# Middle stage of an audio tower: banded filter rows stored 128 columns wide and loaded in two halves, gate and expert weights loaded a stage earlier, packs last, triangular systems in thirds

## What is computed

```
# layer 1: attention of each block with itself
probs = softmax(x @ x.T / 16);   h = probs @ x
# layer 2: h = h + attn(layernorm(h)); 4 heads of 64, chunks of 32 tokens
q, k, v = silu(causal_dwconv(xn @ W, 4 taps));   beta = sigmoid(xn @ Wb)
A = tril(kb @ k.T, -1);  T = inv(eye(32) + A);  u = T @ v_b;  w = T @ kb     # per chunk
# delta rule over the chunks of a sequence with a 64x64 state S
fir_short = causal_dwconv(v, 3 taps);   fir_long = causal_dwconv(v, 63 taps)
gates = softmax(mlp(concat(xn, mean and std of the four branches)))
o = gates . (fir_short, fir_long, delta_out, v);  o = rmsnorm(o) * w;  h += o @ Wo
# layer 3: h = h + ffn(layernorm(h)); 6 experts 256 -> 128 -> 256, top 2 of a router
```

## Time and profile before

| | us |
|---|---|
| median of 3 runs | 2713.1 (2710.72 to 2714.3) |
| the profiled execution, its own time | 2711.45 |
| its span, first to last instruction | 2709.7 |
| PE busy | 2412.4 (89%) |
| DVE busy | 1929.9 (71%) |
| ACT busy | 1377.0 (51%) |
| middle stage, first DMA issue to the first product of the third stage | 764.45 to 932.67 |

### The profile page before, as it was taken

How to read it: one execution, slowest core, us unless ns; L and a number is a source line. 1 busy time by engine, 2 the same in 40 slices (tenths; PEclk the granted TensorE clock), 3 DMA queues, 4 the chain that set the end, 5 groups by cost and what they waited for, 6 DMA issues and landing times.

```text
span 2709.7 us, 53423 instructions
## 1 busy us (share of the span) xinstructions
PE 2412.4 (89%) x21052; PEld 1817.1 (67%) x21052; DVE 1929.9 (71%) x5233; ACT 1377.0 (51%) x2633; POOL 537.6 (20%) x373
## 2 busy tenths in 40 slices
PE   4888888888889689999999999999999999999997
PEld 3666666666568566677767777776777677777764
DVE  3888898998859246667767776777676667656655
ACT  3777777777734224444454444445444544454442
POOL 0333333333310001111111111111111111111111
PEclk9998999999987568999999999999999999999999
DMA  2666666666679702223212221322132223212200
GB/s 79 194 206 204 202 202 207 205 219 206 199 281 345 259 19 90 69 68 112 68 62 102 102 68 62 103 77 68 66 111 89 68 71 109 68 62 92 85 18 18
DMA packets 223162, 334.47 MB, mean 123 GB/s; under 512 B 113857, under 2 KB 190625, under 8 KB 213697
## 3 DMA queue, kind: packets, MB, share of 16 engines
q1 hardware_dynamic: 219744, 309.03, 34.3%
q10 hardware_dynamic: 2304, 12.58, 1.2%
q0 software_dynamic: 864, 9.44, 0.9%
HBM read 191.68 MB, written 164.23 MB: 131 GB/s over the span
## 4 chain that ended last, share of the span: by engine, by line
PE 40%; DVE 16%; ACT 6%; issue 3%; POOL 0%; DVEq 0%
PE bank L1543 6%; PE bank L1474 5%; PE bank L1533 5%; PE bank L1366 4%; PE bank L1485 3%; DVE DL L1875 3%; PE bank L1504 3%; ACT L1680 3%; DVE v_all L1961 3%; PE bank L1478 2%; PE bank L1397 2%; PE bank L1405 2%; PE bank L1452 1%; DVE e L1920 1%; ACT HE L1680 1%
## 5 line engine op out<-in xcount | busy, mean ns | idle before, releaser
L704 DVE SCALAR_TENSOR_TENSOR Y<-bank,convw,Y 128x383 f32<-128x383 f32 (+2 forms) x576 | 314.4, 605 | 7.0 <-ACT Y L580 7.0
L1543 PE MATMUL bank<-w2e,HE 128*128 128x256 f32 x1152 | 289.9, 388 | 12.1 <-DVE v_all L1961 9.2
L1961 DVE SCALAR_TENSOR_TENSOR v_all<-bank,we,v_all 128x256 f32<-128x256 f32 x576 | 242.7, 476 | 79.2 <-PE bank L1543 76.9
L432 PE MATMUL bank<-pb,wqkv 128*128 128x384 f32 x768 | 284.9, 501 | 10.6 <-issue 10.5
L1533 PE MATMUL bank<-v_all,w1e 128*128 128x384 f32 x768 | 285.8, 495 | 1.4 <-ACT HE L1680 1.4
L1841 DVE TENSOR_TENSOR L<-bank,b2g 128x48 f32<-128x48 f32 x32 | 6.6, 208 | 343.7 <-PE bank L1485 343.7
L1543 PEld LDWEIGHTS bank<-w2e,HE 128*128 128x128 f32 x1152 | 208.0, 192 | 49.5 <-issue 16.6
L1474 PE MATMUL bank<-v_all,w1g 128*128 128x384 f32 x512 | 201.8, 517 | 0.4 <-ACT v_all L1672 0.4
L1680 ACT ACTIVATE HE<-bank 128x384 f32<-128x384 f32 x192 | 94.3, 491 | 194.6 <-PE bank L1533 193.8
L432 PEld LDWEIGHTS bank<-pb,wqkv 128*128 128x128 f32 x768 | 137.4, 196 | 83.0 <-issue 24.6
L804 POOL TENSOR_TENSOR RR<-RS,minus_half 128x24 f32<-128x24 f32 x32 | 133.3, 4165 | 267.9 <-DVE RS L753 267.9
(11 more groups left out here) (211 smaller groups left out, 5342.2 us busy)
## 6 DMA issues: line engine op xcount, KB each, us to landing
packa<-pa SPq DMA_DIRECT2D x32, 1932.0 KB, 8.1
v_all<-packa SPq DMA_DIRECT2D x32, 1932.0 KB, 7.8
packb<-pb SPq DMA_DIRECT2D x32, 768.0 KB, 5.9
v_all<-packb SPq DMA_DIRECT2D x32, 768.0 KB, 6.9
toeplitz<-taps SPq DMA_DIRECT2D x128, 190.0 KB, 4.9
toep<-toeplitz SPq DMA_DIRECT2D x32, 760.0 KB, 9.4
packb<-fsk SPq DMA_DIRECT2D x32, 384.0 KB, 2.3
first_stage<-fl SPq DMA_DIRECT2D x32, 384.0 KB, 5.5
```

The costliest lines, as they stand in the source:

```text
L432: mm = pe.matmul(proj_bank[j][:, 0:T], wqkv[:, a, j * P:(j + 1) * P], xnT[:, a, :], start=(a == 0), stop=(a == HALF - 1))
L704: dve.scalar_tensor_tensor(out=Y[:, j, lag:T], in0=proj_bank[j][:, 0:T - lag], scalar=convw[:, j, CK - 1 - lag:CK - lag], in1=Y[:, j, lag: ...
L1543: mm = pe.matmul(expert_bank(b), HE[k % 2][:, b * P:(b + 1) * P], w2e[:, k, :], start=True, stop=True)
L1961: dve.scalar_tensor_tensor(out=HA[s][:, b, :], in0=expert_bank(b), scalar=we[s][:, b, k:k + 1], in1=HA[s][:, b, :], op0=ALU.mult, op1=ALU. ...
```

## The change

- `toeplitz` holds 128 instead of 190 columns a row. A row p below 64 keeps the first 128 columns of its window, one from 64 on the last 128 (the columns left out hold zeros there).
- Each filter group is loaded by two DMAs, 64 rows each: rows 0 to 63 to columns 0 to 127 of `toep`, rows 64 to 127 to columns 62 to 189. Columns 0 to 61 of rows 64 to 127 are cleared once by four DVE memsets, for which PE waits before its first group. The product with the last 62 columns uses rows 64 to 127 alone.
- `w1g` (512 KB) and the six parts of `w1e` (128 KB each) are allocated ahead of the first stage and loaded in its first seven steps that have a sequence c.
- `load_packs` stands behind the last filter load.
- Each set of systems is loaded by three DMAs of 512 KB, issued at given values of `solve_step`; set 0 by three in a row. The stores stay whole.
- A semaphore that nobody waited for (`v_kept`) goes.

```diff
--- before.py
+++ after.py
@@ -99,7 +99,7 @@
             "systems": nc.dram_tensor("systems", [NB * NM * NQ, SC, SC], F32, kind="Internal").ap(),
             "fl": nc.dram_tensor("fl", [NH, P, NB * BLK * DH], F32, kind="Internal").ap(),
             "taps": nc.dram_tensor("taps", [D, 512], F32, kind="Internal").ap(),
-            "toeplitz": nc.dram_tensor("toeplitz", [P, D, TW], F32, kind="Internal").ap(),
+            "toeplitz": nc.dram_tensor("toeplitz", [P, D, P], F32, kind="Internal").ap(),
         }
         c = ctx
         bank = banks()
@@ -113,8 +113,9 @@
         shared = dict(expanded=expanded, NB=NB, dram=dram, bank=bank, ident=ident, upper=upper)
         make_constants(nc, ctx, ident, upper)
         v_all = sb("v_all", [P, D, BLK * NB])
-        first_phase(nc, x, w, shared, v_all)
-        third_phase(nc, w, out, shared, third_phase_weights(nc, ctx), v_all)
+        early = early_weights(nc, ctx)
+        first_phase(nc, x, w, shared, v_all, early)
+        third_phase(nc, w, out, shared, third_phase_weights(nc, ctx, early), v_all)
 
 
 def make_constants(nc, ctx, ident, upper):
@@ -145,7 +146,7 @@
                 sp.sem_inc(g.sem, g.per * g.primed)
 
 
-def first_phase(nc, x, w, shared, v_all):
+def first_phase(nc, x, w, shared, v_all, early):
 
     NB, dram, bank, ident, upper, expanded = (shared[k] for k in ("NB", "dram", "bank", "ident", "upper", "expanded"))
     with ExitStack() as c:
@@ -258,7 +259,6 @@
         kbT0_copied = signal("kbT0_copied")
         kbT1_copied = signal("kbT1_copied")
         at_copied = signal("at_copied", 2)
-        v_kept = signal("v_kept")
         prime(nc, signals)
 
         proj_bank = [bank[n] for n in (3, 4, 5, 3, 4, 5)]
@@ -345,13 +345,22 @@
 
                     for k in range(P // NB):
                         p = c * (P // NB) + k
-                        sp.dma_start(dram["toeplitz"][p], dram["taps"][:, bass.ds(P - 1 - p, TW)]).then_inc(expanded, 16)
+                        sp.dma_start(dram["toeplitz"][p], dram["taps"][:, bass.ds(P - 1 - p + (p // DH) * (FL - 1), P)]).then_inc(expanded, 16)
+
+                def load_early(c):
+                    if c == 0:
+                        sp.dma_start(early["w1g"][:, :, :], w["mlp_w1"][0:D].rearrange("(a p) n -> p a n", a=HALF))\
+                            .then_inc(early["early_loaded"], 16)
+                    elif c <= NE:
+                        sp.dma_start(early["w1e"][:, :, c - 1, :], w["ffn_w1"][c - 1].rearrange("(a p) n -> p a n", a=HALF))\
+                            .then_inc(early["early_loaded"], 16)
 
                 def body(a=None, b=None, c=None, s=0, ahead=True):
                     if a is not None and ahead:
                         load_x(a + 1, 1 - s)
                     if c is not None:
                         expand(c)
+                        load_early(c)
                     if b is not None:
                         store_h(b, 1 - s)
                     if c is not None:
@@ -369,6 +378,7 @@
                 body(NB - 1, NB - 2, NB - 3, 1, ahead=False)
                 body(b=NB - 1, c=NB - 2, s=0)
                 body(c=NB - 1, s=1)
+                sp.wait_ge(early["early_loaded"], 16 * (1 + NE))
                 for s in range(2):
                     sp.wait_ge(*pack_stored[s].before(NB // 2))
                     sp.wait_ge(*h_stored[s].before(NB // 2))
@@ -812,8 +822,7 @@
 
                         pool.wait_ge(*vtok_copied.now(c))
                         for b in range(BLK):
-                            keep = pool.tensor_copy(v_all[:, :, c + b * NB], toks(pa[s], VTOK)[:, b, :])
-                        keep.then_inc(v_kept.sem, 1)
+                            pool.tensor_copy(v_all[:, :, c + b * NB], toks(pa[s], VTOK)[:, b, :])
                     if a is not None:
                         inverse_std(a)
 
@@ -826,11 +835,19 @@
                 body(c=NB - 1, s=1)
 
 
-def third_phase_weights(nc, ctx):
+def early_weights(nc, ctx):
     def sb(name, shape):
         return ctx.enter_context(nc.sbuf_tensor(name, shape, F32))
 
-    w1g = sb("w1g", [P, HALF, MLP])
+    return dict(w1g=sb("w1g", [P, HALF, MLP]), w1e=sb("w1e", [P, HALF, NE, DE]),
+                early_loaded=ctx.enter_context(nc.semaphore("early_loaded")))
+
+
+def third_phase_weights(nc, ctx, early):
+    def sb(name, shape):
+        return ctx.enter_context(nc.sbuf_tensor(name, shape, F32))
+
+    w1g, w1e = early["w1g"], early["w1e"]
     w1s = sb("w1s", [P, MLP])
     b1g = sb("b1g", [P, MC])
     w2g = sb("w2g", [P, MC, 4 * NH])
@@ -840,7 +857,6 @@
     router = sb("router", [P, HALF, NE])
     anchors = sb("anchors", [P, NE, ND])
     rclip = sb("rclip", [P, 1])
-    w1e = sb("w1e", [P, HALF, NE, DE])
     w2e = sb("w2e", [P, NE, D])
     itemp = sb("itemp", [P, NH])
     loaded = ctx.enter_context(nc.semaphore("p3_weights"))
@@ -864,28 +880,24 @@
     if n == 2:
         load(tail["wo"][:, :, :], w["Wo"].rearrange("(a p) n -> p a n", a=HALF))
     if n == 3:
-        load(tail["w1g"][:, :, :], w["mlp_w1"][0:D].rearrange("(a p) n -> p a n", a=HALF))
-    if n == 4:
         load(tail["w1s"][0:GATE_S, :], w["mlp_w1"][D:])
         load(tail["w2g"][:, :, :], w["mlp_w2"].rearrange("(m p) n -> p m n", m=MC))
-    if n == 5:
+    if n == 4:
         load(tail["b2g"][:, :], w["mlp_b2"].partition_broadcast(P))
         load(tail["anchors"][:, :, :].rearrange("p e d -> p (e d)"), w["ffn_anchors"].rearrange("e d -> (e d)").partition_broadcast(P))
-    if n == 6:
+    if n == 5:
         with nc.allow_non_contiguous_dma(reason="a few columns, once"):
             load(tail["b1g"][:, :], w["mlp_b1"].rearrange("(m p) -> p m", m=MC))
-    if n in (7, 8):
+    if n in (6, 7):
         with nc.allow_non_contiguous_dma(reason="a few columns, once"):
-            load(tail["router"][:, n - 7, :], w["ffn_proj_w"][:, (n - 7) * P:(n - 6) * P].rearrange("e p -> p e"))
-    if 9 <= n < 9 + NE:
-        load(tail["w1e"][:, :, n - 9, :], w["ffn_w1"][n - 9].rearrange("(a p) n -> p a n", a=HALF))
-    if n == 9 + NE:
+            load(tail["router"][:, n - 6, :], w["ffn_proj_w"][:, (n - 6) * P:(n - 5) * P].rearrange("e p -> p e"))
+    if n == 8:
         load(tail["w2e"][:, :, :], w["ffn_w2"].rearrange("e p n -> p e n"))
 
 
-WEIGHT_LOADS = 18
+WEIGHT_LOADS = 11
 CLEARED = 3 + 7
-CONSTANTS = 2 + NE - 1
+CONSTANTS = 2 + NE - 1 + 4
 
 
 def second_phase(nc, w, shared, v_all, stage, tail, solve, load_packs, load_factors):
@@ -907,7 +919,7 @@
         toep = [sb(f"toep{s}", [P, CG, TW]) for s in range(NT)]
         solve["X"][0] = sb("X0", [P, SG, SC, SC])
         GI = DH // CG
-        toep_loaded = [signal(f"toep_loaded{s}", 16) for s in range(NT)]
+        toep_loaded = [signal(f"toep_loaded{s}", 32) for s in range(NT)]
         fl_ready = signal("fl_ready", 2, primed=2)
         fl_copied = signal("fl_copied", 2, primed=2)
         prime(nc, signals)
@@ -923,15 +935,16 @@
                 for it in range(groups):
                     if it >= NT:
                         sp.wait_ge(*fl_ready.now(it - NT))
-                    sp.dma_start(toep[it % NT][:, :, :], dram["toeplitz"][:, it * CG:(it + 1) * CG, :])\
-                        .then_inc(toep_loaded[it % NT].sem, 16)
+                    for half in range(2):
+                        rows = slice(half * DH, (half + 1) * DH)
+                        sp.dma_start(toep[it % NT][rows, :, half * (FL - 1):half * (FL - 1) + P],
+                                     dram["toeplitz"][rows, it * CG:(it + 1) * CG, :]).then_inc(toep_loaded[it % NT].sem, 16)
                     if it == NT:
                         for g in tail["signals"]:
                             sp.sem_inc(g.sem, g.per * g.primed)
                     if it > NT:
                         load_third_phase_weight(nc, sp, w, tail, it - NT - 1)
-                    if it == groups - 6:
-                        load_packs(sp)
+                load_packs(sp)
                 load_factors(sp, setup_act)
                 sp.wait_ge(loaded, 16 * WEIGHT_LOADS)
 
@@ -944,6 +957,7 @@
                                   v_all[:, D - 5 * (k + 1):D - 5 * k, :].rearrange("p c n -> p (c n)"), start=True, stop=True)
 
                 dense(5)
+                pe.wait_ge(setup, CONSTANTS)
                 for i in range(0, groups // NT):
                     for s in range(NT):
                         it = i * NT + s
@@ -959,8 +973,8 @@
                                           start=(k == 0), stop=False, skip_group_check=True)
                             for k in range(4):
                                 ch, o = half * 4 + k, k * BLK * NB
-                                mm = pe.matmul(acc[0:TW - P, o + NB:o + BLK * NB], toep[s][:, ch, P:],
-                                               v_all[:, it * CG + ch, 0:(BLK - 1) * NB],
+                                mm = pe.matmul(acc[0:TW - P, o + NB:o + BLK * NB], toep[s][DH:P, ch, P:],
```

(27 more changed lines are left out.)

## The result

The changed kernel takes 2724.1 us (median of 5 runs, 2719.87 to 2727.97); before takes 2713.1 (5 runs, 2708.77 to 2714.3). The ratio is 1.0043, with a 95% interval of 1.0028 to 1.0057. The change makes the kernel slower, by 11.0 us from median to median and 11.7 by the ratio, where 38 us of gain were forecast. The profiled execution took 2727.97 us, 16.5 more than that of before: 4.0 in the first stage (the middle stage begins at 768.45, before at 764.45), 8.4 in the middle stage, 4.2 from the third stage's start on.

A forecast was written before the change was run, and what follows sets the result against it. PE's middle stage was held to lose 42.2 us to two filter-load stalls and their half-clock stretches; with PE ending at 889 and the third stage starting at 895, 37.7 us earlier, 2711.45 became 2673.8, predicted 2675 us, range 2663 to 2700.

The forecast's parts named there:

- Filter rows: Middle-stage filter loads: 1,024 pieces of 512 bytes at 28.7 ns, 1.84 us a group instead of 2.08.
- ledger of 103.9 us: Middle stage: DMA work up to the last filter load, 122.5 us before, 103.9 after; unstalled PE leaves 115.7.
- tight stretch: Middle stage, 790 to 833: DMA work fills 42.6 of 43 us; PE may run dry once, 4 us allowed.
- the cover is 18 us for 7.4 us of data: Middle stage's end: packs issued 13 us ahead of PE's end, needed 5 us behind it; otherwise first products wait some 5 us.
- Packs last: Middle stage: packs behind the last filter load remove SP's 14.3 us wait and 7.4 us of DMA ahead of load 27.
- rival e: Gain given back, for instance by packs or factors that land late: within 0.2% of before; chance 2%.
- the forecast's 895: Start of the third stage, taken as the later of ACT's 894.4 and DVE's 894.1; 37.7 us ahead of 932.67.
- Rival (b): Filter loads: 512-byte pieces cost 47 ns, also for 128 KB HBM stride; third stage at 921, gain 12, 2701 us; 9%.
- Rival (a): Middle stage: PE runs dry more often, one full half-clock stretch and some 5 us of stalls; gain 24, 2689 us; 20%.
- Rival (c): Middle stage: 64-row products let TensorE's clock fall; 2.68 us lost per half-clock group, 2757 us with all 32; 7%.
- the +2 us for the thirds: Middle stage: set 0 in three loads lets DVE end 2 us later, at 893.6; start up to 1 earlier or 5 later.
- A rule against the change: DMA queues take equal turns by piece, so 512-byte filter loads get almost nothing while a set or `fl` store runs.

The follow-up runs named there:

- one_load: Changed kernel with one 128-partition filter load into columns 0 to 127 instead of two of 64 partitions (filter result displaced); 2693.55 us, ratio 0.9924 to before.
- packs_last_only: Kernel before with only the packs moved behind the last filter load; 2692.88 us, ratio 0.9926 to before.
- hbm_stride: Changed kernel with a partition's filter rows 131,584 instead of 131,072 bytes apart in HBM; 2716.23 us, ratio 1.0006 to before.
- wide_whole: Kernel before with only early weights and packs last (190-column filter rows, whole systems); 2686.70 us, ratio 0.9898 to before.
- wide_factors_first: Changed kernel with 190-column filter rows in one load, 128-row products, and factor loads issued ahead of the packs; 2688.50 us, ratio 0.9916 to before.
- deferred: Kernel before with early weights and packs last, plus the fourth systems set and some factor loads moved to the third stage; 2682.14 us, ratio 0.9869.
- two_queues: Changed kernel with filter rows 64 to 127 loaded by ACT on its own queue, SP keeping rows 0 to 63; 2704.50 us, ratio 0.9968 to before.
- halves_only: Kernel before with only the new filter rows (128 columns, two 64-row loads, memsets, 64-row product); 2731.27 us, ratio 1.0066 to before.
- early_only: Kernel before with only the weights loaded in the first stage; 2703.92 us, ratio 0.9976 to before.

## Why the prediction was wrong

**The step that failed is the price of a 512-byte piece**, under "Filter rows": 28.7 ns, 1.84 us a group, "as source and target are of the kind of the large loads". Measured: 41.9 ns, 64 x 41.9 = 2.68 us a group, more than the 2.08 of the wide rows that it replaces. It lay inside the bounds named, 21.9 and 47 ns, but the choice between them looked at bytes and memories and not at which partitions a load touches. The runs show that as the cause: the same pieces cost 29.3 ns when one load covers 128 partitions, 41.9 when loads of 64 come one after the other on a queue, 36.3 when two queues serve the halves; stride and alignment leave 42.2 and 40.1. The estimate of 28.7 was right for loads of 128 partitions, and the trace of before could have shown it: beside other sizes it holds 1,536 pieces of 512 bytes, the loads of `w1e` to 128 partitions, at 27.0 ns on the mean. The Trainium skill states the mechanism ("SBUF — State Buffer", Door 1: The DMA port swizzle): partition bit 6 selects which of two ports of a cluster is used, so 64 neighbouring partitions reach 8 of the 16 ports. Half of the 436 GB/s that the page gives is 218; the trace agrees, with 16 x 512 bytes / 41.9 ns = 196 GB/s and the 180 of the first window. The same page of the Trainium skill ("Can I just issue two DMAs to hit both halves?") says that two concurrent DMAs at partitions 0 and 64 were only 6% faster than a single one. Here two queues against one queue made the pieces 13% shorter, 36.3 against 41.9 ns. No run here counts ports, so that the limit is the ports is the page's reading and not shown.

The half-wide loads slow the others too: up to PE's end POOL's 4,096-byte pieces took 215 ns in the changed kernel and 185 in one_load, the pieces of ACT's stores (6,144 bytes) 299 and 247. The ledger of 103.9 us becomes 32 x 2.68 + 45 = 131 with the first alone, above the 122.5 of before and above the 115.7 that PE needs. The tight stretch, which the prediction saw as "42.6 of 43 us", was then far over: the stall came at the second group, and all else of the PE timeline follows. Unstalled PE would have taken from 775.5 to 889; it took 41.7 us longer, of which the three stalls are 6.8. 11 groups at half clock (7, 2 and 2, by 41.8, 12.0 and 11.6 us between stall and next `dense`) at up to 2.68 us too much are 29, and the `dense` at the end of each stretch, 5.17, 4.72 and 3.94 us instead of 2.52, are 6.3; together 42.

**The second failed step is "the cover is 18 us for 7.4 us of data"** under "Packs last". The data were covered: the first product never waited for `packa`. What was not counted is what stands behind the packs in SP's list. The chance for a gain given back by late packs or factors was put at 2% (rival e), without its price: 8 issues that took 6.3 us before take 23.67 behind packs and slow filter loads, and the third stage starts 14.35 us behind PE, not 5.4 or the forecast's 6. Yet the move itself gains 20 us, as packs_last_only shows; that part of the forecast was right in sign and in cause. In all, the third stage started 50.0 us behind the forecast's 895: 4.0 from the first stage, 37.7 from PE's slower filters and 8.3 from the pause behind them.

**Rival (b)** named the right term, with 47 ns for 41.9, but at 2701 us the wrong sum and, with HBM rows 128 KB apart, the wrong mechanism (hbm_stride). It counted one half-clock stretch where there were three, no slowing of other queues, and the old tail. **Rival (a)** is the way in which PE was hit, short stalls that each cost a stretch. **Rival (c)** fell as it was put: no stretch of 0.50 in the middle stage begins without a stall ahead of it, full clock holds from 828 to 848 and 903 to 931 on filter products alone, and 8 of the short products take 0.66 us, before 0.67. The clock is lost by stalls of 1.67 us as by ones of 10 us. Not every short stall costs it, and here a weaker form of (c) stays open. Where the last products had 128 rows, stalls of 1.35 us (wide_whole), 1.45 and 1.61 (wide_factors_first) left the clock at 1.00, and 1.93 (deferred) and 2.15 (wide_whole) did not. Where they had 64, stalls of 1.15 (one_load) and 1.50 us (two_queues) were already followed by 0.50 (though an idle time of 2.80 us right behind the first `dense` of halves_only was not). So the 64-row products may make the clock easier to lose; no run changes them alone.

Right were: the duration of the 64-row products; 3.31 and 5.99 us a group; DVE not being what ends the stage. The 3.5 us of DMA that the early weights free fit the 6.5 us of early_only, but its interval takes in no gain as well. DVE began `X0` at 778.64, 10.2 us behind the stage's start against 11.5 before, so that the +2 us for the thirds did not show here (with wide rows they cost 4); but it then waited 10.59 us for a constant that ACT makes when PE has done 8 groups, and ended at 904.9 instead of 893.6.

**Open.** The 4.0 us of the first stage: packs_last_only, which changes nothing there, begins its middle stage at 768.98, hbm_stride at 769.39, early_only at 766.42. So the change is not needed for them; that there is only one profile of before leaves it at that. The third stage's 4.2 us: the clock's first stretch at 0.50 doesn't explain them, since it ends 60.4 us behind the stage's start (1005.4) and in before 59.5 (992.2). Whether the DMA engines take turns by piece, as "A rule against the change" has it, no run settles.

## What to carry to other kernels

Where DMA engines bound a stage, ask how many partitions a load covers at once, besides bytes and pieces: here two loads of 64 partitions in a row on one queue cost more (2.68 us a group) than one of 128 with half as many bytes again (2.08). Read busy share and GB/s side by side; a share of 0.91 at 180 GB/s where another stretch makes 390 says that the engines are held up, not short of work. And when a transfer moves to the end of an engine's list, price the issues behind it at what they take with much else under way, since the engine's own end may become the stage's.

## What the runs showed of the hardware

- 512-byte pieces into 64 partitions: 40.1 to 44.6 ns in four kernels; into 128: 29.3 in one_load and 27.0 in before; into both halves by two queues: 33.6 and 39.0. In the changed kernel other queues' pieces take 16 to 21% longer than in one_load.
- An issue of SyncE is not always some 0.3 us: a load of 384 pieces of 128 bytes takes 0.8 us on the mean with little else under way (6.3 / 8), and 2 to 3 us with megabytes of other transfers ahead (16.96 to 23.67 / 8). That it waits for room in a queue is a reading; no run shows the room.
- A PE stall of 1.67 us was followed by 47 us at half clock, 42 of them filter products. In the changed kernel each of the three stretches ended within a `dense` or right at its end, and no kernel here got its clock back on filter products alone:

```profile
822.42 5.17 PE L956 MATMUL bank<-v_all,ident 128*128 128x480 f32 x6
...
861.36 4.72 PE L956 MATMUL bank<-v_all,ident 128*128 128x480 f32 x6
...
900.48 3.94 PE L956 MATMUL bank<-v_all,ident 128*128 128x480 f32 x6
```

  So a stall cost here what lay between it and the next `dense`: 7 groups for the one of 1.67 us at the second group, 2 for that of 3.19.
